# Self-attention of a decoder layer: 26 weight pieces split on GpSimd, bias scaling on ScalarE, low part of the values in the slot of its high part

## The reference, cut to what matters

```
x = layernorm(x + self_attention(x))        # 32 heads of 16, causal, biases bq bk bv bo
x = layernorm(x + cross_attention(x, ctx))  # 32 query heads of 128, 8 key/value heads, rotary positions
x = layernorm(x + ffn(x))                   # 512 -> 1376 -> 512, weights unpacked from 4 bits

q = (x @ Wq.T + bq) ; k = (x @ Wk.T + bk) ; v = (x @ Wv.T + bv)    # heads of 16
att = softmax(where(causal, q k^T / 4, -inf))
self_attention = (att v) @ Wo.T + bo
```

## Time and profile before

| | us |
|---|---|
| median of three runs | 1004.94 (1004.56 to 1010.07) |
| the profiled execution | 1009.34 |
| its span | 1007.5 |
| TensorE matmul busy | 918.1 (91%) |
| VectorE busy | 745.3 (74%) |
| ScalarE busy | 452.2 (45%) |
| GpSimd busy | 367.6 (36%) |
| mean granted clock of TensorE | 0.974 |

### The profile page before, as it was taken

How to read it: one execution, slowest core, us unless ns; L and a number is a source line. 1 busy time by engine, 2 the same in 40 slices (tenths; PEclk the granted TensorE clock), 3 DMA queues, 4 the chain that set the end, 5 groups by cost and what they waited for, 6 DMA issues and landing times.

```text
span 1007.5 us, 17835 instructions
## 1 busy us (share of the span) xinstructions
PE 918.1 (91%) x6552; PEld 521.8 (52%) x6552; DVE 745.3 (74%) x1254; ACT 452.2 (45%) x1271; POOL 367.6 (36%) x330
## 2 busy tenths in 40 slices
PE   3878899788789999979999999998998898999997
PEld 2556677554445555535555555554454443444443
DVE  5587899776587977668697787778888654898343
ACT  3576788641254545345454454534444432333100
POOL 2151122014354554345454445446655212232001
PEclk9898999889999999989999999999999998999999
DMA  6736342300001200122003002032110001220001
GB/s 195 211 143 187 104 127 69 130 4 1 0 2 42 64 1 1 35 72 84 22 1 105 1 13 94 1 129 88 63 48 2 1 1 41 99 96 1 11 32 42
DMA packets 50535, 59.48 MB, mean 59 GB/s; under 512 B 5037, under 2 KB 35728, under 8 KB 50448
## 3 DMA queue, kind: packets, MB, share of 16 engines
q1 hardware_dynamic: 50448, 58.33, 18.0%
HBM read 51.96 MB, written 6.36 MB: 58 GB/s over the span
## 4 chain that ended last, share of the span: by engine, by line
PE 63%; DVE 15%; issue 10%; POOL 4%; ACT 4%; DMA 3%; SPq 2%; POOLq 0%; ACTq 0%; DVEq 0%
PE bank L284 18%; PE bank L285 18%; PE bank L286 18%; DVE rsin L858 3%; PE bank L1258 2%; ACT prob L678 2%; DVE pTl L750 2%; DVE nmax L776 1%; PE bank L1149 1%; POOL res L453 1%; DVE ebias L914 1%; PE bank L1248 1%; PE bank L1247 1%; PE bank L1246 1%; PE bank L1242 1%
## 5 line engine op out<-in xcount | busy, mean ns | idle before, releaser
L460 POOL TENSOR_TENSOR rot<-rcos,rsin 128x512 f32<-128x512 f32 x80 | 102.3, 1278 | 123.7 <-DVE rsin L858 123.6
L678 ACT ACTIVATE prob<-bank,ebias 128x128 f32<-128x128 f32 x256 | 90.3, 364 | 96.6 <-DVE ebias L914 96.6
L472 POOL TENSOR_TENSOR pnrm<-prob,rden 128x512 f32<-128x512 f32 x64 | 66.5, 1040 | 142.5 <-DVE rden L921 142.5
L284 PE MATMUL bank<-aTh,xqh 128*128 128x512 f16 x256 | 99.3, 388 | 12.9 <-DVE rsin L858 9.4
L285 PE MATMUL bank<-aTl,xqh 128*128 128x512 f16 x256 | 99.1, 387 | 0.0
L286 PE MATMUL bank<-aTh,xql 128*128 128x512 f16 x256 | 98.8, 386 | 0.0
L286 PE MATMUL bank<-xoh,o2l 128*128 128x512 f16 x256 | 97.1, 379 | 0.0
L285 PE MATMUL bank<-xol,o2h 128*128 128x512 f16 x256 | 97.1, 379 | 0.0
L284 PE MATMUL bank<-xoh,o2h 128*128 128x512 f16 x256 | 97.1, 379 | 0.0
L565 ACT ACTIVATE prob<-bank,ebias 128x128 f32<-128x128 f32 x256 | 73.5, 380 | 41.6 <-DVE ebias L779 41.2
L520 ACT ACTIVATE pTh<-bank 128x512 f16<-128x512 f32 x128 | 78.4, 612 | 29.7 <-PE bank L1258 15.9
(11 more groups left out here) (159 smaller groups left out, 2463.4 us busy)
## 6 DMA issues: line engine op xcount, KB each, us to landing
tst<-tables SPq DMA_DIRECT2D x11, 768.0 KB, 5.2
xqs<-in_xwq SPq DMA_DIRECT2D x8, 1024.0 KB, 7.8
xos<-in_xwo SPq DMA_DIRECT2D x8, 1024.0 KB, 5.6
qst<-in_fq SPq DMA_DIRECT2D x11, 384.0 KB, 3.4
kstk<-stack SPq DMA_DIRECT2D x48, 64.0 KB, 2.3
qstk<-stack SPq DMA_DIRECT2D x24, 128.0 KB, 2.6
stT<-in_xT SPq DMA_DIRECT2D x4, 512.0 KB, 7.4
stT<-in_ctxT SPq DMA_DIRECT2D x1, 2048.0 KB, 8.7
```

The source lines that it names most:

```text
L284: pe.matmul(out_ap, ah, bh, start=first, stop=False)
L460: nc.gpsimd.tensor_tensor(rot[:, r % 2, :], rcos[:, r % 2, :], rsin[:, r % 2, :], ALU.add).then_inc(rope_rot, 1)
L472: nc.gpsimd.tensor_tensor(pnrm[:, v % 2, :].rearrange("p (h k) -> p h k", h=QH), prob[:, v % 2, :].rearrange("p (h k) -> p h k", h=QH), rd ...
L678: last = nc.scalar.activation(prob[:, v % 2, j * S:(j + 1) * S], bank[2 + v % 2][:, j * S:(j + 1) * S], ACT.Exp, bias=ebias[:, v % 2, j:j ...
```

## The change

- `weight_plan` moves the slots of the pieces of groups 0 and 1 and of the output weights of group 0. New tables place six pieces of `w1` (chunks 2 and 3) and the four of `wo1`.
- GpSimd makes both parts of these 26 pieces (6 + 4 + 12 + 4) with three operations each, every one waiting for the one before: scale the float32 source in place, cast it to the high part, subtract. ScalarE's and VectorE's work on them is gone.
- GpSimd's loop begins with `FIRST`: the key and query splits stand in the slots in which ScalarE writes their source, and the eight residual additions in slots 16 to 23, one in each.
- The bias of the exponentials of the self-attention is scaled on ScalarE, from VectorE's row maximum.
- The low part of the values is made on VectorE in the slot of its high part, one slot earlier.

```diff
-    qkv = {0: [24, 26, 28, 30, 32, 34], 1: [38, 40, 42, 44, 46, 48]}
-    out = {0: [50, 52, 54, 55], 1: [T0 + 2, T0 + 3, T0 + 4, T0 + 5]}
+    qkv = {0: [26, 28, 29, 30, 34, 36], 1: [38, 42, 44, 45, 46, 50]}
+    out = {0: [52, 53, 54, 58], 1: [T0 + 2, T0 + 3, T0 + 4, T0 + 5]}
...
+W1_SLOT = {(2, 0): 4, (2, 1): 5, (2, 2): 6, (3, 0): 20, (3, 1): 21, (3, 2): 22}
+WO1_SLOT = {0: 10, 1: 12, 2: 13, 3: 14}
+POOL_QKV, POOL_OUT = (0, 1), (0,)
...
-            for j in range(BLOCKS):
-                split_keys(j)
-                split_queries(j)
-                if j == 1:
+            def add_bias(b):
+                if b == 0:
                     pool.wait_ge(res_in, 32)
-                    for b in range(NB):
-                        nc.gpsimd.tensor_tensor(res[:, b, :], res[:, b, :], bo_bc[:, :], ALU.add).then_inc(res_ready, 1)
+                nc.gpsimd.tensor_tensor(res[:, b, :], res[:, b, :], bo_bc[:, :], ALU.add).then_inc(res_ready, 1)
...
+            def split_piece(hi, lo, src, lo_done):
+                nonlocal pieces_done
+                pieces_done += 1
+                nc.gpsimd.tensor_scalar(src, src, 2.0 ** E_W, None, ALU.mult).then_inc(piece_scaled, 1)
+                pool.wait_ge(piece_scaled, pieces_done)
+                nc.gpsimd.tensor_copy(hi, src).then_inc(piece_hi, 1)
+                pool.wait_ge(piece_hi, pieces_done)
+                nc.gpsimd.tensor_tensor(lo, src, hi, ALU.subtract).then_inc(lo_done, 1)
+
+            def w1_piece(c, i):
+                pool.wait_ge(w1_in, (c + 1) * 48)
+                pool.wait_ge(v1_psum, NHALF * (c - 1))
+                split_piece(w1h[:, c % 2, i, :, :], w1l[:, c % 2, i, :, :], w1s[:, i, :, :], w1_lo)
...
-            for t in range(FILLS[0][0], END + 6):
-                v = t - T0
+            for t in range(FIRST, END + 6):
+                j, n, v = t // TILES1, t % TILES1, t - T0
+                if j + 2 < BLOCKS and n == 6:
+                    split_keys(j + 2)
+                if j + 1 < BLOCKS and n == 0 and t >= -TILES1:
+                    split_queries(j + 1)
+                pieces(t)
+                if 16 <= t < 16 + NB:
+                    add_bias(t - 16)
...
             def exps1(u):
+                act.wait_ge(nmax_done, u + 1)
+                if u >= 2:
+                    act.wait_ge(exp_done, u - 1)
+                split_hi(ebias[:, u % 2, :], nmax[:, u % 2, :], -2 * E_QK - 2).then_inc(ebias_done, 1)
                 act.wait_ge(ebias_done, u + 1)
...
-                dve.wait_ge(nmax_done, u + 1)
-                nc.vector.tensor_scalar(ebias[:, u % 2, :], nmax[:, u % 2, :], 2.0 ** (-2 * E_QK) / 4, None,
-                                        ALU.mult).then_inc(ebias_done, 1)
...
-                if before + 1 < BLOCKS and m == 4 and t - 1 > -TILES1:
-                    v1_split_lo(before + 1)
+                if j + 1 < BLOCKS and n == 4 and t > -TILES1:
+                    v1_split_lo(j + 1)
```

More of the change, by code:

```diff
@@ L252, in decoder_kernel @@
             sem("consts_ready"), sem("mask_ready"), sem("res_ready"), sem("zeroed"), sem("power_set"))
-        scaled_bias, wo1_hi, wo1_ready = sem("scaled_bias"), sem("wo1_hi"), sem("wo1_ready")
+        scaled_bias, wo1_ready = sem("scaled_bias"), sem("wo1_ready")
         w1_hi, w1_lo = sem("w1_hi"), sem("w1_lo")
+        piece_scaled, piece_hi = sem("piece_scaled"), sem("piece_hi")
         k1_psum, q1_psum, v1_psum = sem("k1_psum"), sem("q1_psum"), sem("v1_psum")
@@ new lines, in _ @@
+            pieces_done = 0
+            def split_piece(hi, lo, src, lo_done):
[6 more added lines that the diff above has]
+                nc.gpsimd.tensor_tensor(lo, src, hi, ALU.subtract).then_inc(lo_done, 1)
@@ new lines, in w1_piece, with wo1_piece, qkv_piece @@
+            def w1_piece(c, i):
+                pool.wait_ge(w1_in, (c + 1) * 48)
+                pool.wait_ge(v1_psum, NHALF * (c - 1))
+                split_piece(w1h[:, c % 2, i, :, :], w1l[:, c % 2, i, :, :], w1s[:, i, :, :], w1_lo)
+            def wo1_piece(k):
+                pool.wait_ge(wo1_in, 16)
+                split_piece(woTh[:, k, :], woTl[:, k, :], woTs[:, k, :], wo1_ready)
+            def qkv_piece(g, piece):
+                pool.wait_ge(xq_in, 16 * (g + 1))
+                if piece < 4:
+                    split_piece(xqh[:, g % 2, piece, :], xql[:, g % 2, piece, :], xqs[:, piece, :], xq_lo)
+                else:
+                    pool.wait_ge(xkv_in, 32 * (g + 1))
+                    src, hi, lo = ((xks, xkh, xkl), (xvs, xvh, xvl))[piece - 4]
+                    split_piece(hi[:, g % 2, :, :], lo[:, g % 2, :, :], src[:, :, :], xq_lo)
@@ new lines, in o_piece, with pieces @@
+            def o_piece(g, h):
+                pool.wait_ge(xo_in, 16 * (g + 1))
+                split_piece(xoh[:, g % 2, h, :], xol[:, g % 2, h, :], xos[:, h, :], xo_lo)
+            def pieces(t):
+                for (c, i), slot in W1_SLOT.items():
+                    if slot == t:
+                        w1_piece(c, i)
+                for k, slot in WO1_SLOT.items():
+                    if slot == t:
+                        wo1_piece(k)
+                for g in POOL_QKV:
+                    for piece in range(6):
+                        if QKV_SLOT[g][piece] == t:
+                            qkv_piece(g, piece)
+                for g in POOL_OUT:
+                    for h in range(QH):
+                        if OUT_SLOT[g][h] == t:
+                            o_piece(g, h)
@@ L619, in weight_pieces @@
             def weight_pieces(t):
-                for g in range(G):
+                for g in range(len(POOL_QKV), G):
                     for piece in range(6):
@@ L623, in weight_pieces @@
                             qkv_hi(g, piece)
-                for g in range(G):
+                for g in range(len(POOL_OUT), G):
                     for h in range(QH):
@@ L663, in _ @@
                     w1_split_hi(1, t + 3)
-                if j in (1, 3) and n in (1, 3, 5):
-                    w1_split_hi((j + 3) // 2, n // 2)
                 if j in (0, 1) and n in (3, 7):
                     ctx_split_hi(2 * j + n // 4)
-                if j == 2 and n % 2 == 1:
-                    wo1_split_hi(n // 2)
                 weight_pieces(t)
@@ L755, in w1_split_lo @@
                 split_lo(w1l[:, c % 2, i, :, :], w1s[:, i, :, :], w1h[:, c % 2, i, :, :], E_W).then_inc(w1_lo, 1)
-            def wo1_split_lo(k):
-                dve.wait_ge(wo1_hi, k + 1)
-                split_lo(woTl[:, k, :], woTs[:, k, :], woTh[:, k, :], E_W).then_inc(wo1_ready, 1)
             def ctx_split_lo(k):
@@ L884, in qkv_lo @@
                                  (xkh, xvh)[piece - 4][:, g % 2, :, :]))
-                dve.wait_ge(xq_hi, 6 * g + piece + 1)
+                dve.wait_ge(xq_hi, 6 * (g - len(POOL_QKV)) + piece + 1)
                 split_lo(dst, src, hi, E_W).then_inc(xq_lo, 1)
             def o_weight_lo(g, h):
-                dve.wait_ge(xo_hi, 4 * g + h + 1)
+                dve.wait_ge(xo_hi, QH * (g - len(POOL_OUT)) + h + 1)
                 split_lo(xol[:, g % 2, h, :], xos[:, h, :], xoh[:, g % 2, h, :], E_W).then_inc(xo_lo, 1)
             def weight_pieces(t):
-                for g in range(G):
+                for g in range(len(POOL_QKV), G):
                     for piece in range(6):
@@ L1015, in _ @@
                 before, m = (t - 1) // TILES1, (t - 1) % TILES1
-                if before + 1 < BLOCKS and m == 4 and t - 1 > -TILES1:
-                    v1_split_lo(before + 1)
+                if j + 1 < BLOCKS and n == 4 and t > -TILES1:
+                    v1_split_lo(j + 1)
                 if t in (-2, -1, 0):
                     w1_split_lo(1, t + 2)
-                if before in (1, 3) and m in (1, 3, 5):
-                    w1_split_lo((before + 3) // 2, m // 2)
                 if before in (0, 1) and m in (3, 7):
                     ctx_split_lo(2 * before + m // 4)
-                if before == 2 and m % 2 == 1:
-                    wo1_split_lo(m // 2)
                 weight_pieces(t - 1)
```

5 lines of the change are left out of this document (removed).

## The result

The changed kernel takes 996.98 us (median of six runs, 994.07 to 1000.22) against 1008.88 for the kernel before (six runs, 1004.56 to 1013.08). The ratio is 0.9872, interval [0.9844, 0.9899]: faster by 1.3%, about half of what was forecast, and outside the range. The profiled execution took 996.39 us against 1009.34.

What follows compares the result with a forecast made beforehand. TensorE and VectorE were taken to set the self-attention blocks' pace, with a GpSimd-caused stall in block 1. Block gains of 24.7 less 1.7 gave 23.0 us: 986.3 from the profile, 981.9 from the median, taken as 983; range 974 to 994.

Steps and rivals of the forecast that it cites:

- taken at 0.8, nearer the one-input row: GpSimd's in-place scaling of a 128x512 float32 piece: 0.8 us assumed, between 0.69 and 1.47.
- p: Time of one weight piece on GpSimd (scaling, cast, subtraction): 2.6 us, bounds 2.5 and 4.4.
- holds: GpSimd's queue meets block 4's need for stacked operands at 109.9 as long as p is up to 2.9.
- Rival B: GpSimd's queue late at block 4, p between 2.9 and 4.4; at 3.4 a 5 us wait, 988; chance 0.18.
- the forecast 107.1: Stacked operands of block 4 ready at 81.1 + 10p = 107.1 us, against a need at 109.9.
- Cost taken 0: VectorE's stand for the early values is made up in two slots: 0, at worst 1.1 us in six blocks.
- at ScalarE's pace: Block 6, without keys and queries, paced by ScalarE: 16.6 us, 2.1 won.
- Blocks 1 and 2: Self-attention blocks forecast at 19.7 us (10.4 won) and 18.5 us (2.4 won).
- the scaling on ScalarE: Each of the 64 bias scalings moved to ScalarE takes 0.19 to 0.3 us.
- VectorE's 1.1 us stand: In the values' slot VectorE waits 1.1 us for ScalarE's high part, with TensorE not waiting.
- the 1.7 set aside for the clock: Taken off the 24.7 us sum for one 1.2 GHz stretch somewhere in blocks 1 to 5.
- rival C: VectorE's relief not turned into time; only block 1's stall and the values' waits return, 16.1 us: 990; chance 0.10.

Runs made afterwards that it cites:

- the control: The changed kernel run once more with nothing altered: 998.16 us, ratio 0.9908 to the kernel before.
- a_noscale: The changed kernel with GpSimd's scaling of the 26 pieces left out, so it computes something else: 991.28 us, ratio 0.9845 to the kernel before.
- a_bcast: The changed kernel with GpSimd's scaling written as a product with a broadcast column instead of a constant: 991.47 us in one run.
- a_w3back: The changed kernel with three of the 26 pieces given back to ScalarE and VectorE at their old slots: 995.47 us, ratio 0.987 to the kernel before.
- the broadcast kernel: The changed kernel with GpSimd's scaling as a product with a broadcast column, timed twice: 991.47 and 991.62 us.
- c_best: The changed kernel with broadcast-column scaling, low part of the values late in blocks 0 and 6, and context parts two slots later: 987.99 us, ratio 0.9784.
- c_bcast: The changed kernel with GpSimd's scaling as a product with a broadcast column, timed again: 991.62 us, ratio 0.9819 to the kernel before.
- b_resadd: The kernel before with only GpSimd's list reordered (splits and residual additions), no piece moved: 1004.81 us, ratio 0.9944.
- b_res_eb_v1: The changed kernel without the 26 pieces on GpSimd, their work left on ScalarE and VectorE at the old slots: 1007.97 us, ratio 0.9963.

## Why the prediction was wrong

**The scaling was mis-sized.** The term "taken at 0.8, nearer the one-input row" measured 1.49, just over its upper bound of 1.47 (which was a mean over additions of which the longest took 2.24 us; their median is 1.28). So p was 3.4 and not 2.6, beyond the 2.9 up to which the queue "holds". Rival B had the step, "the first slot of block 4 waits 10 x 0.5 = 5 us", against 4.41 measured; the 1.4 us of low clock behind it were not in B, and its time, 988, was missed as well. Blocks 3 and 4 together missed by 6.0 us (4.7 in the control). Both ways of shortening the piece (`a_noscale`, `a_bcast`) and giving pieces back (`a_w3back`) take the wait away.

The 4.41 are near B's 5 partly by luck. In the changed kernel's timelines the queue begins at 49.20 and not 51; the ten pieces take 35.9 us, 3.59 each with three disturbed operations among them; the six split pairs take 10.9; the eight additions take 9.8 and not 11.8; and from the query split to its use it is 9.0 us and not 7.5. That gives 114.8 in place of the forecast 107.1, against a need at 110.4. In the 9.0 us SyncE's issues of the stacked reads take 3.61 and 2.24 us, where they took 2.75 and 1.38 a block earlier; why is not shown.

**"Cost taken 0" for the early values failed in block 6.** It was argued from a block with projections ("TensorE needs these only after another 2.5 us slot"), and block 6 has no keys and queries. Its forecast of 16.6 "at ScalarE's pace" is reached (16.43, 16.71) only with the late part. The cost is 2.0 us against the forecast, over the "at worst 1.1 us" of the prediction. Where there are queries the move is right: 0.9 us in blocks 4 and 5.

**Blocks 1 and 2**, 1.3 and 1.6 us over. In block 1 (and 0) VectorE stood 2.05 us and not 1.1, since ScalarE has a context part before the values' high part; TensorE waits 1.28 us in block 1 for the low part of the probabilities behind that stand. In block 2 the stand is 1.10 us, as forecast. But the low half of the fourth context part (2.08 us at 75.08) falls in block 2, where the forecast had none. How much of the 1.6 us it is, no run shows: the broadcast kernel has this block at 19.42 and at 18.34 in its two profiles. Moving the context parts won nothing, for GpSimd's queue was next, and in `c_best`, with the cheaper pieces, it still is. What blocks 1 and 2 would take without it is open.

**What was right:** block 5 (18.2 for 18.4); no wait of TensorE for the values; the scaling on ScalarE at 0.20 to 0.24 us; VectorE's 1.1 us stand in the blocks without a context part before it. That block 0 (18.8 for 18.7) and the eighth window (2.2 won for 2.0) agree is worth less: block 0 is 19.84 in the control, and the eighth window, 73.17 before, is 73.23, 73.32 and 73.09 us in `a_noscale`, `a_w3back` and `c_bcast`. The misses, 6.0 + 2.9 + 2.0, less the 1.7 set aside for the clock and some tenths won elsewhere, are the 8.6 us between 23.0 and 14.4.

**Right place, wrong owner.** The forecast and rival C both gave block 1 its 10.4 us for the additions' new place; alone it brings 6.8 there and 3.3 in the stage (`b_resadd`). The parts need one another: in block 2 the additions cost 3.0 us beside the old VectorE work. With the bias scaling gone to ScalarE and the values early, and the weight pieces still there (`b_res_eb_v1`), that block is back at 21.02.

**Against which time.** 983 was worked from a median of three runs, 1004.94; with six it is 1008.88, and the profiled 1009.34 was typical. From that own time the forecast was 986.3: 3 of the 14 us of miss are this choice. Of the 10.1 us between 986.3 and the profiled 996.39, 8.6 are the stage, and 1.5 are left of the stretch behind it (4.1 longer) and the early start (2.6).

## What to carry to other kernels

When work is moved to an idle engine, its list has dates as well as a load: write down, for every hand-over in the list, when it is needed and how many operations stand before it, and what price per operation breaks it. If that breaking price lies within the bounds of a cost that the trace doesn't show, give the miss a large chance: here 2.9 us lay between the bounds of 2.5 and 4.4, and the miss got 0.18. A wait that is free beside a busy TensorE has to be priced again in the block where TensorE has less to do.

## What the hardware showed

On GpSimd a product of a 128x512 float32 tile with a constant, in place, takes 1.49 us, with a broadcast column 1.04, the sum of two tiles 1.28, the subtraction with float16 output 1.16, a cast to float16 0.61. Of the operations with one tensor input the cast was the cheapest of all and the scaling the dearest, and rewriting the scaling as a product of two operands was worth 5 to 6 us in blocks 3 and 4.

A small operation of VectorE on 128x4 values in SBUF took 257 ns on average in the kernel before and 475 with GpSimd working on the pieces; on ScalarE the same scaling took 220.

One kernel, profiled twice, had a stage of 204.5 and 207.0 us, and work that no kernel changed took 747.5 to 751.6 us.
